# Gate logits of a four-stage transformer block by fp32 products with the turned rows stationary, placed behind the heads' products two tiles at a time

## What is computed

```
def _L1_ffn_ref(x, wg, w1, b1, w2, b2):
    ...
    logits = xt.astype(jnp.float32) @ wg.astype(jnp.float32)
    scores = jax.nn.softmax(logits, axis=-1)
    gvals, gidx = jax.lax.top_k(scores, K)
    ...
    loc = jnp.cumsum(m, axis=0) - 1 + offset[None, :]
    ...
    disp = jnp.zeros((E, cap, D), x.dtype).at[e_flat, p_flat].add(x_rep * kmask[:, None])
    h = jax.nn.gelu(jnp.einsum('ecd,edh->ech', disp, w1) + b1[:, None, :], approximate=False)
```

## Time and profile before

| what | us |
|---|---|
| median of 3 runs | 536.81 |
| lowest and highest | 535.91, 539.48 |
| the profiled execution | 542.02 |
| its span, first to last instruction | 540.3 |
| granted TensorE clock, mean over the span | 0.956 of full speed |

### The profile page before, as it was taken

One profiled execution on the slowest core, in us unless ns is written; L12 is line 12 of the kernel. 1 busy time (PEld: TensorE's weight loads), 2 busy tenths in 40 slices (PEclk: granted clock), 3 DMA queues, 4 the chain that ended last, 5 costly groups with the idle time before them and its releaser, 6 DMA issues.

```text
span 540.3 us, 8651 instructions
## 1 busy us (share of the span) xinstructions
PE 494.9 (92%) x3269; PEld 417.9 (77%) x3269; DVE 398.0 (74%) x754; ACT 259.9 (48%) x408; POOL 147.4 (27%) x124
## 2 busy tenths in 40 slices
PE   6999989989998899899999847899999999999991
PEld 4687768877887777687877623898999999999991
DVE  3867999999998768769878877748684766767441
ACT  2465667676863655445455413425434433434120
POOL 2444100010000302212012203720525537273263
PEclk9689979999999999889999997999999999999997
DMA  7313100000000011210311431213537456462031
GB/s 236 109 43 87 39 0 2 1 1 1 2 0 2 2 38 40 79 57 22 106 53 41 156 118 36 83 15 92 158 87 170 110 141 131 143 149 57 8 40 19
DMA packets 37163, 36.07 MB, mean 67 GB/s; under 512 B 6456, under 2 KB 35970, under 8 KB 36994
## 3 DMA queue, kind: packets, MB, share of 16 engines
q1 hardware_dynamic: 30661, 27.65, 16.3%
q0 software_dynamic: 6144, 7.66, 8.7%
q10 hardware_dynamic: 317, 0.21, 0.1%
HBM read 27.70 MB, written 8.39 MB: 67 GB/s over the span
## 4 chain that ended last, share of the span: by engine, by line
PE 56%; DVE 27%; issue 7%; ACT 3%; SPq 2%; DMA 2%; POOL 1%; DVEq 0%; ACTq 0%; POOLq 0%
PE PS L1398 12%; PE PS L1400 12%; PE PS L1399 12%; PE PS L1773 5%; PE PS L1715 4%; DVE tmp L1082 3%; DVE tmp L1069 3%; PE PS L1640 3%; DVE hT_lo L1090 3%; PE PS L1416 2%; PE PS L1782 2%; SPq L515 2%; DVE st L935 2%; DVE xT_lo L959 2%; DVE tmp L1057 1%
## 5 line engine op out<-in xcount | busy, mean ns | idle before, releaser
L1398 PE MATMUL PS<-w_hi,hT_hi 128*128 128x256 f32 x384 | 112.0, 292 | 1.3 <-DVE hT_lo L1090 1.1
L1399 PE MATMUL PS<-w_lo,hT_hi 128*128 128x256 f32 x384 | 110.3, 287 | 0.0
L1400 PE MATMUL PS<-w_hi,hT_lo 128*128 128x256 f32 x384 | 110.3, 287 | 0.0
L907 ACT ACTIVATE tmp<-PS,biasT 128x512 f32<-128x512 f32 (+1 forms) x80 | 43.9, 600 | 112.5 <-PE PS L1400 112.5
L648 POOL DMA_INDIRECT out<-tmp,dst_idx x32 | 55.8, 1743 | 99.8 <-DVE tmp L1354 93.1
L1398 PE MATMUL PS<-xT_hi,w_hi 128*128 128x512 f32 (+1 forms) x224 | 81.3, 363 | 0.4 <-DVE xT_lo L959 0.4
L1399 PE MATMUL PS<-xT_lo,w_hi 128*128 128x512 f32 (+1 forms) x224 | 80.7, 360 | 0.0
L1400 PE MATMUL PS<-xT_hi,w_lo 128*128 128x512 f32 (+1 forms) x224 | 80.5, 359 | 0.0
L1398 PEld LDWEIGHTS PS<-w_hi,hT_hi 128*128 128x128 f32 x384 | 75.1, 195 | 5.0 <-issue 2.6
L1399 PEld LDWEIGHTS PS<-w_lo,hT_hi 128*128 128x128 f32 x384 | 75.3, 196 | 0.9
L1400 PEld LDWEIGHTS PS<-w_hi,hT_lo 128*128 128x128 f32 x384 | 75.3, 196 | 0.0
(11 more groups left out here) (235 smaller groups left out, 895.4 us busy)
## 6 DMA issues: line engine op xcount, KB each, us to landing
w_raw<-in_L_ffn_w SPq DMA_DIRECT2D x72, 256.0 KB
residual<-in_x SPq DMA_DIRECT2D x4, 512.0 KB, 5.4
out<-residual SPq DMA_DIRECT2D x3, 512.0 KB, 4.2
normed_rows<-xn SPq DMA_DIRECT2D x3, 512.0 KB, 2.9
kv<-in_L_ffn_b SPq DMA_DIRECT2D x1, 1024.0 KB, 6.5
tmp<-in_L_xattn_Wq SPq DMA_DIRECT2D x2, 256.0 KB, 5.5
out<-residual SPq DMA_DIRECT2D x2, 256.0 KB, 4.2
normed_rows<-xn SPq DMA_DIRECT2D x2, 256.0 KB, 2.2
```

Of the source, the lines that this page charges most:

```text
L907: act.activation(gD[:, G % 2, f, 0:P * n], H[:, G % 2, f, 0:P * n], ACT.Gelu, bias=biasT[:, col:col + 1]).then_inc(e_gelu, 1)
L1398: pe.matmul(o, lh, rh, start=start, stop=False, skip_group_check=skip)
L1399: pe.matmul(o, lh, rl, start=False, stop=False, skip_group_check=skip)
L1400: return pe.matmul(o, ll, rh, start=False, stop=stop, skip_group_check=skip)
```

## The change

The logits are now one fp32 product for each tile and half of the columns: the turned rows, 128x128, are stationary, and the gate's 128x8 matrix (`wg_raw`, unsplit) moves. The result comes out as rows, so that `logits_columns`, `copy_logits`, `logits_rows`, the split of the gate's matrix and the semaphores lgT_ready and lgT_copied go away, and with them `x_lo` for the five pieces. ScalarE's copy (`x3_copy`) is one plain fp32 copy into room beside the keys (pieces 0, 1, 2, 4) or in tmp (piece 3). Pieces 0 and 1 are done in halves of two tiles, at t = 8 and 9 and at t = 12 and 13, behind PV and ahead of the output product, into the unused end of PV's bank; VectorE takes both halves in `normalise` of the tile done at t = 9 or 13. Piece 2 follows the turning of piece 3 in t = 16; piece 3 follows the loop. VectorE takes piece 2's logits and does its max and index ahead of the last statistics, its marks later. `keep_warm` goes from 8 and 5 products to 12 and 4. On SyncE's queue the experts' b2 goes behind the last two saves and waits for the last logits. The core of the diff:

```diff
+LOGITS_AT = {8: (0, 0), 9: (0, 2), 12: (1, 0), 13: (1, 2)}
...
+        x3T_last = view(7616, KD, 256)
...
+        x3T = [xT_even, xT_even, xT_even, x3T_last, xT_even]
...
+            if c == 2:
+                return LG
+            return PS[:, 4 if c == 3 else 7, 288:320].rearrange("p (t e) -> p t e", t=4)
...
-            sp.wait_ge(c_scores, 3 * NT)
+            save(3)
+            save(4)
+            sp.wait_ge(lg_ready, len(PIECES) - 2)
             sp.dma_start(b2e_bc, b2.rearrange("e d -> (e d)").partition_broadcast(P)
...
-            save(3)
-            save(4)
...
+            def x3_copy(c):
+
+                r = round_of(3, c)
+                act.wait_ge(tr_ready, r + 1)
+                if c in (1, 2):
+                    act.wait_ge(c_pv, 4 * c + 5)
+                elif c == 4:
+                    act.wait_ge(lg_ready, 1)
+                n = P * tiles_of(r)[1]
+                act.activation(x3T[c][:, :, 0:n], turned_bank(r)[:, :, 0:n], ACT.Copy).then_inc(xlo_ready, 1)
...
-                link(dve.reciprocal(rc, pv[:, :, P:P + HH]))
+                mark_at = mark(dve.reciprocal(rc, pv[:, :, P:P + HH]))
+                if s in (8, 12):
+                    take_logits((s - 8) // 4)
+                dve.wait_ge(dve_chain, mark_at)
...
-                if t in TURN_AT:
-                    x_lo(round_of(3, TURN_AT[t]))
...
-                if t in COLUMNS_AT:
-                    take_logits(COLUMNS_AT[t])
...
-            x_lo(r3)
+            take_logits(2)
+            top_values(2)
             last_stats(r4)
             apply(r4)
-            take_logits(2)
             take_logits(3)
+            link(marks_of(2))
             link(top_two(3))
-            x_lo(r4)
-            link(top_two(2))
...
+            def logits_of(c, first=0):
 
                 r = round_of(3, c)
                 pe.wait_ge(xlo_ready, r + 1)
-                if c < 3:
+                if c == 2:
                     T_free()
                 elif c == 4:
...
                     pe.wait_ge(c_conc, NT)
...
+                for i in range(first, first + 2 if c < 2 else PIECES[c][1]):
+                    for k in range(KD):
+                        ins = pe.matmul(logit_rows_bank(c)[:, i, :], x3T[c][:, k, P * i:P * i + P], wg_raw[:, k, :],
+                                        start=(k == 0), stop=(k == KD - 1))
...
-                if t in COLUMNS_AT:
-                    logits_columns(COLUMNS_AT[t])
...
+                    if t in LOGITS_AT:
+                        ins = logits_of(*LOGITS_AT[t])
                     ins.then_inc(c_pv, 1)
...
-                if t in COLUMNS_AT:
-                    logits_rows(COLUMNS_AT[t])
-
-
-            logits_columns(2)
-            logits_columns(3)
-            logits_rows(2)
-            logits_rows(3)
-            keep_warm(5, 8)
+                    logits_of(2).then_inc(lg_ready, 1)
+
+
+            logits_of(3).then_inc(lg_ready, 1)
+            keep_warm(5, 12)
             transpose_x(round_of(3, 4))
-            keep_warm(5, 5)
-            logits_columns(4)
-            logits_rows(4)
+            keep_warm(5, 4)
+            logits_of(4).then_inc(lg_ready, 1)
```

More of the change, by code:

```diff
@@ L422, in round_used @@
             elif s == 3:
-                eng.wait_ge(lgT_ready, c + 1)
+                if c < 2:
+                    eng.wait_ge(c_pv, 4 * c + 9)
+                else:
+                    eng.wait_ge(lg_ready, c - 1)
             else:
@@ L956, in x_lo @@
             def x_lo(r):
-                dve.wait_ge(xhi_ready, r - NC + 1)
+                dve.wait_ge(xhi_ready, sum(1 for q in range(NC, r + 1) if q >= NR or ROUNDS[q][0] < 3))
                 n = P * tiles_of(r)[1]
@@ L1170, in take_logits, with top_values @@
             def take_logits(c):
-                dve.wait_ge(lg_ready, c + 1)
+                if c < 2:
+                    dve.wait_ge(c_pv, 4 * c + 9)
+                else:
+                    dve.wait_ge(lg_ready, c - 1)
                 first, n = PIECES[c]
                 dve.tensor_copy(logits[:, first:first + n, :], logit_rows_bank(c)[:, 0:n, :]).then_inc(lg_copied, 1)
-            def top_two(c):
+            def top_values(c):
                 first, n = PIECES[c]
-                here = slice(first, first + n)
                 dve.wait_ge(lg_copied, c + 1)
@@ L1185, in top_two, with marks_of @@
                 link(ins)
+            def marks_of(c):
+                first, n = PIECES[c]
+                here = slice(first, first + n)
                 link(dve.tensor_copy(ixf[:, :, here], topi[:, here, 0:2].bitcast(U32).rearrange("p t k -> p k t")))
@@ L1193, in top_two @@
                 return ins
+            def top_two(c):
+                top_values(c)
+                return marks_of(c)
             for t in range(NT + 2):
@@ L1422, in xT @@
                 return xT_hi[:, r % 2, k, a:a + n], xT_lo[:, r % 2, k, a:a + n]
-            turned, queries, logit_chunks, logit_rows = [0], [0], [0], [0]
+            turned, queries, logit_rows = [0], [0], [0]
             def T_free():
@@ L1671, in _ @@
             pe.wait_ge(late_loaded, 48)
-            def logits_columns(c):
+            def logits_of(c, first=0):
                 r = round_of(3, c)
                 pe.wait_ge(xlo_ready, r + 1)
-                if c < 3:
+                if c == 2:
                     T_free()
                 elif c == 4:
-                    pe.wait_ge(lgT_copied, 4)
-                n = P * PIECES[c][1]
-                for k in range(KD):
-                    ins = split_mm(logit_columns_bank(c)[:, 0:n], (wg_hi[:, k, :], wg_lo[:, k, :]), xT(r, k, 0, n),
-                                   k == 0, k == KD - 1)
-                ins.then_inc(lgT_ready, 1)
-                logit_chunks[0] += 1
-            def logits_rows(c):
-                pe.wait_ge(lgT_copied, c + 1)
-                if c == 3:
-                    pe.wait_ge(c_conc, NT)
-                elif c == 4:
-                    pe.wait_ge(lg_copied, 4)
-                for i in range(PIECES[c][1]):
-                    ins = pe.transpose(logit_rows_bank(c)[:, i, :], lgT[0:NE, P * i:P * i + P], ident[0:NE, 0:NE])
-                ins.then_inc(lg_ready, 1)
-                logit_rows[0] += 1
+                    pe.wait_ge(c_conc, NT)
+                for i in range(first, first + 2 if c < 2 else PIECES[c][1]):
+                    for k in range(KD):
+                        ins = pe.matmul(logit_rows_bank(c)[:, i, :], x3T[c][:, k, P * i:P * i + P], wg_raw[:, k, :],
+                                        start=(k == 0), stop=(k == KD - 1))
+                if c == 2:
+                    logit_rows[0] = 3
+                return ins
             def turn_heads(s):
```

33 lines of the change are left out of this document (5 added, 28 removed).

## The result

| what | us |
|---|---|
| changed kernel, median of 4 runs | 548.55 (543.35 to 549.76) |
| kernel before on the same chip, median of 4 runs | 538.14 (535.91 to 539.93) |
| ratio, 95% interval | 1.018, 1.0126 to 1.0235 |
| changed kernel, its profiled execution, its span | 547.48, 545.7 |
| granted TensorE clock, mean over the span | 0.952 |

The change makes the kernel about 10 us slower; 536.1 had been forecast, with 539.5 as the upper end.

What follows compares the result with a forecast made beforehand. TensorE work ahead of the turned heads was taken as the bound, VectorE second. Loop -0.3 and last take -0.61 gave -0.9, taken as -0.7 for issue gaps: 536.81 to 536.1 us; own range 535.2 to 537.1, with rivals 534.0 to 539.5.

Steps and rivals of the forecast that it cites:

- What bounds the loop: Attention loop: TensorE work ahead of turned heads is paid in full; work after PV hides at most 0.16 us.
- The price of a pass: New fp32 logits products: two passes each, 0.116 us a pass, so 0.93 us for a group of eight.
- t = 8's step: First logits group, between PV and output product at t = 8: output product and all behind it late by 0.77 us.
- The rival of short passes: Logits passes take 0.083 us each, +0.50 instead of +0.77 a group; 534.1 us in all; chance 0.15.
- The step that failed: Pieces 0 and 1 at t = 9, 12, 13: old products removed, new passes added; -0.3 us at t = 14.
- this very collision for L951 at t = 16: Last piece's rows on VectorE, started earlier, would still sit behind GpSimd's L583, which runs from 303.62 to 305.98.
- L1115 at 290.57: VectorE's row needed by the exponentials of t = 14, forecast at 290.57 rather than 290.86; exponentials -0.29 us.
- The rival of the other side: TensorE's clock falls in the tail by about 311: +3 us on the forecast, 539.1 us; chance 0.27.
- +2.16: Tail: turned heads of tile 15 late by 2.16 us, behind the third piece's logits and a copy they wait for.
- The sum of -0.61: Tail: turns of the last piece +0.73 us, then 2.48 instead of 3.82 to the last take, which comes 0.61 earlier.
- I give it nothing, and 0.5 at most: t = 16: dropping x_lo ahead of the normalising rows (L951) gains nothing, at most 0.5 us.
- All comes back: Rival: all removed VectorE and TensorE work counts as on the path, near 5 us; 532 us; chance 0.03.

Runs made afterwards that it cites:

- e_tail: Changed kernel with the third piece's logits moved back behind the loop and their take, max and index behind the last apply; 545.83 us, ratio 1.0157.
- e_gate: Changed kernel with GpSimd's low parts at t = 9 and 13 waiting for that iteration's residual add; 542.70 us, ratio 1.0065.
- after: The changed kernel itself, as first measured against the kernel before; median 548.55 us, ratio 1.018, profiled run 547.48 us.
- e_gate_tail: Changed kernel with GpSimd's waits at t = 9 and 13 and the tail's old order of logits restored; 540.38 us, ratio 1.0022.
- e_warm: Changed kernel with seven more warming products in the tail, around tile 15's turned heads and ahead of the third piece's logits; 543.27 us, ratio 1.0123.
- e_gateall_tail: Changed kernel with the tail's old order restored and GpSimd's low parts of units 2 to 7 waiting for their tile's residual add; 535.76 us, ratio 0.9969.
- b_gate: Kernel before the change, with GpSimd's low parts of units 2 to 7 waiting for their tile's residual add; 534.84 us, ratio 0.9955.
- e_ahead: Changed kernel with the logits of pieces 0 and 1 ahead of PV instead of behind it; 543.75 us, ratio 1.0101.

## Why the prediction was wrong

**What bounds the loop** was read rightly: what stands ahead of the turned heads is paid, what stands behind PV is late in the output product. Balanced as I balanced it, the loop should end 0.3 us earlier at t = 14; with the adds unblocked it ends where it did (69.24 against 69.23). The sum was fair, for the path that it followed.

**The price of a pass** was 0.116 and is 0.101 (239.20 to 240.01 for eight). The rule of the Trainium skill, "TensorE: Matmul & The Clock Gate", section "LDWEIGHTS (loading the stationary operand)", gave an estimate of 107 ns; the trace has 101 here, and 107 for the third piece's 16 passes in e_tail (1.71 us from the first to the next group), so the rule was nearer than my row. The groups cost 0.81 instead of 0.93 us; t = 8's step became 0.62 longer (7.48 to 8.10 in e_gate), not 0.77. The rival of short passes was thus half right and worth nothing.

**The step that failed** is the one at t = 9 and at t = 12, 13. I moved the exponentials (-0.37 at t = 9) and the output product (+0.13) and asked only which of TensorE and VectorE would be waited for. Each also releases something else. The exponentials release ScalarE's high half and with it L583; the output product releases L1165 and L1167. L1167 started 0.55 us ahead of L583, and my own two figures leave 0.05 of that at t = 9. At t = 13 they give -0.94 for the turned heads against -0.17 for the output product, which is more than the 0.55. Measured, the add starts 0.29 and 0.07 behind L582. I had named this very collision for L951 at t = 16, from the row, and did not look for other instructions beside L583; "L1115 at 290.57" was 0.29 earlier than before; counted from the residual add of t = 7, it came 3.3 us later, by the two blocks (1.50 and 1.71, below). The rule that I cited for it holds here too: by the Trainium skill, "SBUF — State Buffer", section "Who interferes with whom", one of the two engines keeps the port pair for a whole instruction, and both blocked adds end 0.28 us behind L582 (251.66 against 251.38, and 285.93 against 285.65).

The price of the step, from differences of the starts of residual adds between after and e_gate_tail: 1.50 us for the block at t = 9 (17.20 against 15.70 from t = 8 to 10), 1.71 at t = 13 (15.86 against 14.15 from t = 12 to 14), and 3.86 for the halved clock behind it (t = 14 to 16). The larger half is the clock's.

**The rival of the other side**, the clock in the tail, happened, with its place and nearly its price: half clock from 312 to 322, and 4.05 us in the tail (16.84 against 12.79 in e_warm), for which I had put 3. Against the kernel before the tail is 3.95 longer, where forecast and rival together made 2.4. I gave it 0.27, since the clock had stayed full at 307 with TensorE busy 0.57 of a microsecond. At 310 to 311 it was busy 0.52, and the clock fell at 312. One stretch that was let pass was weak evidence, with a chain of waits on both sides of it. And the rival was only ever priced for the tail; that a VectorE delay in the loop would do the same to TensorE was not among the cases, so the range ended at 539.5.

**The rest of the tail's sum.** The heads of tile 15 came 2.63 us late (the adds of t = 16 and 17 are 5.25 apart in e_warm, 2.62 before), where I had +2.16. From the last L949's end to the last take it is 2.56 us in e_warm (316.00 to 318.56), where I had 2.53. The sum of -0.61 came out as -0.10 there, with seven warming products more. No run has the new order at full clock without them.

**t = 16.** "I give it nothing, and 0.5 at most": L949 was blocked as forecast (2.76 us), and freeing it is worth 0.31.

**All comes back**, at 532, was given 0.03 and is refuted by e_gateall_tail against b_gate.

## What to carry to other kernels

When a change moves two events against each other, list for each what *else* it releases, on every engine, and look in the trace for pairs that already stand close: half a microsecond decided here whether an operation took 0.48 or 2.5 us. A wait of another engine that costs nothing by itself (GpSimd, idle for most of the time) can pin such an order down, and is worth trying by itself: it was all that gained here. An idle stretch of TensorE is to be priced with the half-speed stretch that can follow, 3 to 4 us each time here, and not with its own length alone; and one profile shows whether the clock fell in that execution, not how often it does.

## What the runs showed of the hardware

- An fp32 `scalar_tensor_tensor` of 128x256 with all inputs in SBUF took 2.35 to 2.56 us beside GpSimd's 2.35-us subtraction, against 0.48 alone, and two `tensor_scalar` 2.76 against 0.73. Not every operation is held: three `bn_stats` (L935) took 1.08 beside L583 in the kernel before (0.36 each, as elsewhere: four in 1.40).
- Once at 1.2 GHz, TensorE stayed there for about 10 us in both places of the changed kernel, from 292 to 302 busy all the time, from 312 to 322 nearly so. It was 6.5 us in the kernel before (226.5 to 233) and 3 in e_ahead (275 to 278), also at work all the time: the length is not fixed.
- The same idle time did not always bring the clock down: of ten profiles in which TensorE idled 1.3 us at t = 5 to 6, two have a fall behind it.
- The same code in the tail took 11.60 and 15.26 us in two executions of nearly the same kernel, by the clock alone. A single profile of such a stretch says little about its price.
